# Thirty-two-column tiles for a second mix and an inverse transform, quarter tiles for the last transform

## The chip, the cores and the metric

The kernel runs on one core of one Trainium2 chip. The time is device microseconds (us) of one execution. TensorE is named PE in the profile and its weight loads PEld; VectorE is DVE, ScalarE is ACT, GpSimd is POOL, and the queue that issues the transfers is SP.

## The reference, cut to what matters

Four spectral mixers run one after the other on an array x of 2 images, 64 x 64 positions and 384 channels, all in float32. The second is followed by a token MLP.

```python
xf = rfft2(x, axes=(1, 2)).reshape(B, H, W // 2 + 1, 8, 48)      # 8 blocks of 48 channels
o1 = act(complex_mix(xf, w1) + b1)                               # relu; gelu in layer 1
o2 = complex_mix(o1, w2) + b2                                    # the "second mix"
o2 = softshrink(o2, 0.01)                                        # not in layer 1
y  = irfft2(o2, s=(H, W), axes=(1, 2)) + x
# layer 1 only: LayerNorm ahead, and behind it y + mlp(layernorm(y)), hidden size 1536
```

In layer 1 only 32 of the 64 row frequencies are kept.

## The kernel before

The work on the spectral layers goes by groups g: one block of 48 channels of one layer with both images, so 8 groups a layer and 32 in all. Layers 0, 2 and 3 are "full" (64 row frequencies, 66 columns of the spectrum a group, cut into 9 slots t of 6 or 8 columns); layer 1 is the "norm" layer (4 slots of 16 columns). The program has three spectral stretches: layer 0, layer 1, and layers 2 and 3 together; the token MLP stands between the second and the third.

One group passes through these steps. f1 (line 504) transforms rows, 64x64 tiles of the array, four in use at once. f2 (line 523) transforms columns, with 128 rows and 48 columns in each half of the array. m1 (line 537) is the first mix; ACT applies the activation into h (line 772). m2 (line 555, or 565 in the norm layer) is the second mix: the slot's h is the stationary operand, 64 columns of it a matmul, and the result goes to one of two banks, 4 and 7. In a full layer DVE limits it (clamp, line 928) and subtracts in four pieces of 64 partitions into u (line 934); in the norm layer DVE copies half and ACT half (lines 939, 783). f5 (line 586) is the inverse column transform, six chunks of 8 channels a group: u is stationary, 64 columns a matmul, two matmuls a channel, one for each half of the array. ACT moves the result to v (line 792). f6 (line 602) is the last transform, eight chunks of 8 image rows a group: 128 rows by 64 columns, two matmuls a chunk; DVE adds it to the residual in xs (line 959) and, in layer 0, takes statistics (line 971). SP stores a pair of groups (a unit of 96 channels) in eight transfers and loads a later unit in eight.

The order on each engine is written out by hand. On PE a slot t of group g is: m1 of slot t-1; one f6 chunk of group g-2; f2 of slot t; where due, f1 of group g+1 (slots 0, 3, 6) and f5 of group g-1 (slots 2 to 7); m2 of slot t-1. PE waits in m2 for the eviction of the slot before last (`spread_of(n - 1)`), and in f6 for DVE's addition of the chunk before. The last two groups of a stretch are drained with two banks in turn (`drains`).

Every instruction of PE is in the program text, unrolled, in the spectral stretches; the MLP is a loop. A float32 matmul of the source appears in the profile as two matmul records and two weight loads.

Of the kernel before, what the change touches and what calls it, by code (L numbers as in the profile page):

```python
# [10 lines left out]
P = 128  # L11
# [35 lines left out]
C_ID, C_D5, C_D5H, C_D6, C_COLS = [C_SIGN + SIGNS + P * n for n in range(5)]  # L47
# [11 lines left out]
class Layer:  # L59

    def __init__(self, index, kh, forward, inverse, act, shrink, norm):
# [3 lines left out]
        self.spread = 2 * BATCH if self.full else BATCH  # L65
        self.first_rows = 1 if self.full else 0
# [37 lines left out]
def spread_of(count):  # L104

    return sum(layer_of(g).spread for g, _ in GROUPS[:count])


def imag_of(count):

    return sum(BATCH for g, _ in GROUPS[:count] if layer_of(g).norm)
# [8 lines left out]
ROW_CHUNKS = [(g, k) for g in range(LAYERS * BLOCKS) for k in range(ROWCHUNKS)]  # L120


def row_bank(g, k):
    return 1 if drains(g, k) and k % 2 else 0


def rows_to_clear(g, k):

    n = ROWCHUNKS * g + k
    earlier = [m for m in range(n) if row_bank(*ROW_CHUNKS[m]) == row_bank(g, k)]  # L130
    return earlier[-1] + 1 if earlier else 0
# [63 lines left out]
def build(nc, x, consts, spectral, lncols, ln1, cols, w1, w2, b2, out):  # L195
    with ExitStack() as ctx:
# [30 lines left out]
        with ExitStack() as scope:  # L227
# [10 lines left out]
            u = sb("u", [P, 2, BLOCK, SPAN + BATCH])  # L238
# [35 lines left out]
        F1_BANKS, M2_BANKS, F6_BANKS = (0, 1), (4, 7), (6, 0)  # L274
        F2_BANK, M1_BANK, F5_BANK = 2, 3, 5
# [14 lines left out]
        u_imag, z_shared = sem("u_imag"), sem("z_shared")  # L290
        centred, xn_ready, rows_ready, sum_ready = sem("centred"), sem("xn_ready"), sem("rows_ready"), sem("sum_ready")
        gained, zf_part, u_part, col_ready = sem("gained"), sem("zf_part"), sem("u_part"), sem("col_ready")
# [52 lines left out]
        def _(sp):  # L345
# [24 lines left out]
            def store_unit(unit):  # L370

                for part in range(PARTS):
                    sp.wait_ge(res_ready, ROWCHUNKS * (2 * unit + 1) + PART_ROWS // ROWCHUNK * (part + 1))
# [103 lines left out]
        def _(pe):  # L477

            def f1(g, k):
# [17 lines left out]
                if leads(g) and g and k == 1:  # L497
                    pe.wait_ge(res_ready, ROWCHUNKS * g)
# [42 lines left out]
            def m2(g, t):  # L541
# [4 lines left out]
                if n >= 2:  # L546
                    pe.wait_ge(u_ready, spread_of(n - 1))
                bank = M2_BANKS[n % 2]
# [11 lines left out]
                if imag_of(n - 1):  # L560
                    pe.wait_ge(u_imag, imag_of(n - 1))
                for q in range(size // BATCH):
                    for a in range(2):
                        col = READY_SECOND + a * BLOCK
                        mm = pe.matmul(ps[a * SIDE:(a + 1) * SIDE, bank, q * BLOCK:(q + 1) * BLOCK],  # L565
                                       h[0:ROWS, n % 2, q * SIDE:(q + 1) * SIDE],
                                       mix[0:ROWS, g % 2, col:col + BLOCK], start=True, stop=True)
                mm.then_inc(m2_done, 1)

            def f5(g, k, bank=F5_BANK, reuse=1):  # L570
# [3 lines left out]
                if k == 0:  # L574
                    if g == 0:
                        pe.wait_ge(s_const, 16)
                    pe.wait_ge(u_ready, spread_of(groups_before(g + 1)))
                    if L.norm:
                        pe.wait_ge(u_imag, imag_of(groups_before(g + 1)))
# [4 lines left out]
                for c in range(CHAN):  # L584
                    for a in range(2):
# [748 lines left out]
```

## Time and profile before

| | |
|---|---|
| time, median of 3 runs | 2082.43 us (2081.65 to 2084.39) |
| profiled execution, its own time | 2080.81 us |
| its span | 2079.0 us |
| PE busy | 1934.2 us, 93% |
| DVE busy | 1175.1 us, 57% |
| ACT busy | 1011.0 us, 49% |
| transfers | 141.05 MB, mean 68 GB/s |
| matmul records | 31104, and as many weight loads |

Matmuls overlap each other, so a record's mean time is longer than the step from one to the next, and a busy PE is not PE at its peak. The word "issue" in the profile is time in which an engine waited for nothing that the profile shows.

### The profile page before, as it was taken

The numbers are of one execution on the slowest core, as the hardware profiler recorded it, in microseconds if no ns is written. First come the engines' busy times: TensorE is split into PE (matmuls) and PEld (weight loads), VectorE is DVE, ScalarE is ACT, GpSimd is POOL, SyncE is SP. The second block draws the span as 40 slices with busy tenths as digits, with TensorE's granted clock in tenths as the row PEclk, the third lists the DMA queues.
The fourth block names the chain that finished last, engine by engine and source line by source line (L and its number), as shares of the span: only waits on it lengthen the run. The fifth ranks groups of instructions, "written<-read, shape, count | busy, mean of one in ns | idle before, by whom it ended". The sixth has DMA issues, their size and how long they took to land.

```text
span 2079.0 us, 68971 instructions
## 1 busy us (share of the span) xinstructions
PE 1934.2 (93%) x31104; PEld 1581.3 (76%) x31104; DVE 1175.1 (57%) x2480; ACT 1011.0 (49%) x1644; POOL 434.7 (21%) x425
## 2 busy tenths in 40 slices
PE   5999995698998999999999999999899999999997
PEld 4777672576776999999999999999677777777774
DVE  3687887987855433333333333332467667666675
ACT  3766545576753333333333333333466556655652
POOL 3212103975721000000000000000321121211200
PEclk9999996799998999999999999999999999999998
DMA  9424728307444111111111111114813555457214
GB/s 169 92 49 84 128 58 140 59 8 125 117 103 98 31 31 31 31 30 30 30 30 30 30 30 30 30 31 73 130 16 68 91 101 103 70 86 127 60 36 95
DMA packets 299701, 141.05 MB, mean 68 GB/s; under 512 B 275760, under 2 KB 298032, under 8 KB 299440
## 3 DMA queue, kind: packets, MB, share of 16 engines
q1 hardware_dynamic: 299440, 137.08, 35.9%
q8 instruction: 224, 3.67, 0.8%
q14 instruction: 37, 0.30, 0.0%
HBM read 74.14 MB, written 62.91 MB: 66 GB/s over the span
## 4 chain that ended last, share of the span: by engine, by line
PE 81%; DVE 9%; ACT 3%; issue 2%; POOL 2%; DMA 2%; SPq 1%; DVEq 0%; POOLq 0%; ACTq 0%
PE ps L690 19%; PE ps L675 19%; PE ps L523 9%; PE ps L586 8%; PE ps L537 8%; PE ps L602 7%; PE ps L555 5%; PE ps L504 4%; DVE u L934 3%; DVE st L971 2%; PE ps L565 1%; DVE xs L959 1%; PE ps L660 1%; ACT zf L749 1%; POOL xs L1180 1%
## 5 line engine op out<-in xcount | busy, mean ns | idle before, releaser
L1083 DVE TENSOR_TENSOR gl<-g,gh 128x512 fp32r<-128x512 f32 x192 | 156.8, 817 | 476.4 <-ACT gh L869 476.4
L934 DVE TENSOR_TENSOR u<-ps,clamp 64x192 f32<-64x192 f32 (+1 forms) x864 | 377.0, 436 | 27.7
L866 ACT ACTIVATE g<-ps,colp 128x512 f32<-128x512 f32 x192 | 132.3, 689 | 529.4 <-PE ps L675 529.4
L523 PEld LDWEIGHTS ps<-const,z 128*48 128x48 f32 x8384 | 266.6, 124 | 117.2 <-issue 107.2
L729 ACT ACTIVATE z<-ps 64x512 f32<-64x512 f32 x366 | 234.6, 641 | 113.4 <-PE ps L504 106.6
L523 PE MATMUL ps<-const,z 128*48 128x64 f32 (+1 forms) x8384 | 271.5, 217 | 14.0 <-issue 9.0
L1170 POOL COPY xn<-xs 128x512 f32<-128x512 f32 x144 | 151.2, 1088 | 552.7 <-PE ps L504 364.3
L690 PE MATMUL ps<-w2h,gh 128*128 128x384 f32 x768 | 261.8, 341 | 0.0
L690 PE MATMUL ps<-w2h,gl 128*128 128x384 f32 x768 | 258.5, 337 | 0.0
L690 PE MATMUL ps<-w2l,gh 128*128 128x384 f32 x768 | 257.5, 335 | 0.0
L537 PE MATMUL ps<-zf,w 112*64 112x512 f32 (+2 forms) x992 | 248.3, 574 | 5.9 <-ACT zf L749 1.3
L602 PE MATMUL ps<-v,const 128*64 128x384 f32 x1024 | 219.0, 507 | 21.8 <-DVE xs L959 19.4
L928 DVE TENSOR_SCALAR clamp<-ps 128x384 f32<-128x384 f32 (+1 forms) x216 | 112.6, 521 | 219.3 <-PE ps L555 218.6
L586 PE MATMUL ps<-const,u 128*64 128x64 f32 x6144 | 219.4, 225 | 13.5 <-DVE u L939 6.4
L675 PE MATMUL ps<-mth,w1h 128*128 128x512 f32 x576 | 225.0, 391 | 4.0 <-DVE mtl L1071 4.0
L675 PE MATMUL ps<-mth,w1l 128*128 128x512 f32 x576 | 228.1, 396 | 0.0
L675 PE MATMUL ps<-mtl,w1h 128*128 128x512 f32 x576 | 227.8, 396 | 0.0
L772 ACT ACTIVATE h<-ps,w 113x512 f32<-113x512 f32 (+1 forms) x248 | 162.7, 656 | 122.5 <-PE ps L537 120.1
L586 PEld LDWEIGHTS ps<-const,u 128*64 128x64 f32 x6144 | 199.8, 139 | 29.1 <-ACT v L792 7.5
L749 ACT ACTIVATE zf<-ps 112x512 f32<-112x512 f32 (+1 forms) x216 | 121.3, 561 | 145.1 <-PE ps L523 144.7
L555 PE MATMUL ps<-w,h 113*64 113x96 f32 x3168 | 173.8, 248 | 10.5 <-issue 6.2
L602 PEld LDWEIGHTS ps<-v,const 128*64 128x64 f32 x1024 | 71.2, 139 | 142.8 <-issue 74.1
(70 smaller groups left out, 2516.2 us busy)
## 6 DMA issues: line engine op xcount, KB each, us to landing
after<-xs SPq DMA_DIRECT2D x96, 384.0 KB, 5.4
xs<-after SPq DMA_DIRECT2D x94, 384.0 KB, 8.9
after<-om SPq DMA_DIRECT2D x32, 384.0 KB, 4.3
out<-xs SPq DMA_DIRECT2D x32, 384.0 KB, 5.4
xm<-after SPq DMA_DIRECT2D x30, 384.0 KB, 6.3
xs<-in_x SPq DMA_DIRECT2D x24, 384.0 KB, 8.4
wstage<-in_spectral SPq DMA_DIRECT2D x16, 210.0 KB, 5.7
xs<-in_x SPq DMA_DIRECT2D x4, 768.0 KB, 11.9
```

Of the source, the lines that this page charges most:

```text
L523: mm = pe.matmul(ps[a * SIDE:a * SIDE + BLOCK, F2_BANK, n * L.kh:(n + 1) * L.kh], z[:, g % 2, slot, :], basis(col + a * SIDE, L.kh), start ...
L537: mm = pe.matmul(ps[rows, M1_BANK, 0:width], w[unit % 2][0:MIX, g % 2, rows], zf[0:MIX, n % 2, 0:width], start=True, stop=True)
L555: mm = pe.matmul(ps[b * SIDE:(b + 1) * SIDE, bank, p * PAIR:(p + 1) * PAIR], h[0:ROWS, n % 2, c * SIDE:(c + 1) * SIDE], mix[0:ROWS, g % 2, ...
L586: mm = pe.matmul(ps[a * SIDE:(a + 1) * SIDE, bank, c * SIDE:(c + 1) * SIDE], u[:, g % 2, k * CHAN + c, BATCH * a:BATCH * a + SPAN], basis( ...
L602: mm = pe.matmul(ps[a * SIDE:(a + 1) * SIDE, F6_BANKS[row_bank(g, k)], 0:ROWCHUNK * BLOCK], basis(C_D6 + a * SIDE, SIDE), v[:, g % 2, rows ...
L675: mm = pe.matmul(ps[:, MM1_BANKS[n % 2], :], a[:, at], b[r][:, k, :], start=k == 0 and m == 0, stop=k == KC - 1 and m == 2)
L690: mm = pe.matmul(ps[:, MM2_BANKS[j], 0:CHANNELS], a[:, n % 4, part], b[:, at], start=n == 0 and m == 0, stop=n == HC - 1 and m == 2)
L729: act.activation(to, data, ACT.Copy, scale=layer_of(g).forward).then_inc(z_ready, 1)
L772: act.activation(h[0:ROWS, n % 2, 0:width], ps[0:ROWS, M1_BANK, 0:width], L.act, bias=w[g // 2 % 2][0:ROWS, g % 2, READY_BIAS:W_ALL]).then ...
L934: dve.tensor_tensor(u[to, g % 2, :, start + b:start + size:BATCH], whole, limited, ALU.subtract).then_inc(u_ready, 1)
L1083: dve.tensor_tensor(gl[:, n % 4, :], g[:, n % 2, :], gh[:, n % 4, :], ALU.subtract).then_inc(g_low, 1)
L1170: pool.tensor_copy(xn[:, n % RING], channels(g, k)).then_inc(xt_ready, 1)
```

## The change

Second mix: each matmul covers 32 stationary columns instead of 64 and one half (48) of the 96 output columns, so a column of the slot takes four matmuls, one on each quarter of the array's columns; the result lies with real and imaginary part on the partitions, images side by side. One bank, 4, takes every slot, and PE waits for the eviction of the slot just before. DVE then subtracts in one instruction of 128 partitions; in the norm layer ACT copies all of it in one, and DVE only adds the mean term. Inverse column transform: 32 stationary columns a matmul, four matmuls a channel instead of two. Last transform: except in the drains, two chunks (sixteen rows) a call, each image on its own half of the array's rows, four 64x64 tiles in banks 6 and 7; DVE adds in four pieces of 64 partitions. Calls of f6 move: in a full layer to slots 0, 1, 4 and 8, behind f2 and ahead of f1. Layout constants follow.

```diff
-        F1_BANKS, M2_BANKS, F6_BANKS = (0, 1), (4, 7), (6, 0)
-        F2_BANK, M1_BANK, F5_BANK = 2, 3, 5
+        F1_BANKS, F6_BANKS = (0, 1), (6, 7)
+        F2_BANK, M1_BANK, M2_BANK, F5_BANK = 2, 3, 4, 5
...
 def rows_at(g, t):
...
     if not layer_of(g).full:
-        return [(g - 2, 2 * t), (g - 2, 2 * t + 1)]
-    if t == layer_of(g).n - 1:
-        return [(g - 1, 0)]
-    return [(g - 2, t + 1)] if t < ROWCHUNKS - 1 else []
+        return [(g - 2, 2 * t)]
+    return {0: [(g - 2, 2)], 1: [(g - 2, 4)], 4: [(g - 2, 6)], layer_of(g).n - 1: [(g - 1, 0)]}.get(t, [])
...
                 if L.full:
                     for c in range(size):
-                        p, b = c // BATCH, c % BATCH
                         col = READY_SECOND if start + c < SPAN else MINUS
-                        mm = pe.matmul(ps[b * SIDE:(b + 1) * SIDE, bank, p * PAIR:(p + 1) * PAIR],
-                                       h[0:ROWS, n % 2, c * SIDE:(c + 1) * SIDE],
-                                       mix[0:ROWS, g % 2, col:col + PAIR], start=True, stop=True)
+                        for a in range(2):
+                            for k in (0, HALF):
+                                mm = pe.matmul(ps[a * SIDE + k:a * SIDE + k + HALF, bank, c * BLOCK:(c + 1) * BLOCK],
+                                               h[0:ROWS, n % 2, c * SIDE + k:c * SIDE + k + HALF],
+                                               mix[0:ROWS, g % 2, col + a * BLOCK:col + (a + 1) * BLOCK],
+                                               start=True, stop=True)
...
                 for q in range(size // BATCH):
-                    for a in range(2):
-                        col = READY_SECOND + a * BLOCK
-                        mm = pe.matmul(ps[a * SIDE:(a + 1) * SIDE, bank, q * BLOCK:(q + 1) * BLOCK],
-                                       h[0:ROWS, n % 2, q * SIDE:(q + 1) * SIDE],
-                                       mix[0:ROWS, g % 2, col:col + BLOCK], start=True, stop=True)
+                    for b in range(BATCH):
+                        for a in range(2):
+                            col, to = READY_SECOND + a * BLOCK, b * SIDE + a * HALF
+                            mm = pe.matmul(ps[to:to + HALF, bank, q * BLOCK:(q + 1) * BLOCK],
+                                           h[0:ROWS, n % 2, (q * BATCH + b) * HALF:(q * BATCH + b + 1) * HALF],
+                                           mix[0:ROWS, g % 2, col:col + BLOCK], start=True, stop=True)
...
                 for c in range(CHAN):
-                    for a in range(2):
-                        mm = pe.matmul(ps[a * SIDE:(a + 1) * SIDE, bank, c * SIDE:(c + 1) * SIDE],
-                                       u[:, g % 2, k * CHAN + c, BATCH * a:BATCH * a + SPAN],
-                                       basis((C_D5 if L.full else C_D5H) + a * SIDE, SIDE),
-                                       start=True, stop=True)
+                    for b in range(BATCH):
+                        for a in range(2):
+                            to = b * SIDE + a * HALF
+                            mm = pe.matmul(ps[to:to + HALF, bank, c * SIDE:(c + 1) * SIDE],
+                                           u[:, g % 2, k * CHAN + c, b if L.full else 0, a:a + HALF],
+                                           basis(C_D5 + a * SIDE if L.full else C_D5H + (b * 2 + a) * SIDE, SIDE),
+                                           start=True, stop=True)
...
+                for c in range(2):
+                    rows = slice((k + c) * ROWCHUNK, (k + c + 1) * ROWCHUNK)
+                    for b in range(BATCH):
+                        mine = slice(b * SIDE, (b + 1) * SIDE)
+                        mm = pe.matmul(ps[c * SIDE:(c + 1) * SIDE, F6_BANKS[b], 0:ROWCHUNK * BLOCK],
+                                       const[mine, C_D6 + b * SIDE:C_D6 + (b + 1) * SIDE],
+                                       v[mine, g % 2, rows, :].rearrange("p h c -> p (h c)"), start=True, stop=True)
+                mm.then_inc(f6_done, 2)
...
-                    for b, a in ((0, 0), (0, 1), (1, 1), (1, 0)):
-                        mine, to = slice(b * SIDE, (b + 1) * SIDE), slice(a * SIDE, (a + 1) * SIDE)
-                        whole, limited = (d[mine].rearrange("p (s a c) -> p a c s", a=2, c=BLOCK)[:, a]
-                                          for d in (data, part))
-                        dve.tensor_tensor(u[to, g % 2, :, start + b:start + size:BATCH], whole, limited,
-                                          ALU.subtract).then_inc(u_ready, 1)
+                    whole, limited = (d.rearrange("p (k b c) -> p c b k", b=BATCH, c=BLOCK) for d in (data, part))
+                    first = start // BATCH
+                    dve.tensor_tensor(u[:, g % 2, :, :, first:first + size // BATCH], whole, limited,
+                                      ALU.subtract).then_inc(u_ready, 1)
...
+                dve.wait_ge(f6_done, n + 2)
+                for c in range(2):
+                    for b in range(BATCH):
+                        to = residual(g, (k + c) * ROWCHUNK, ROWCHUNK)[b * SIDE:(b + 1) * SIDE]
+                        data = ps[c * SIDE:(c + 1) * SIDE, F6_BANKS[b], 0:ROWCHUNK * BLOCK]
+                        dve.tensor_tensor(to, data.rearrange("p (h c) -> p h c", c=BLOCK), to, ALU.add).then_inc(res_ready, 1)
```

## Rows read from the trace of the kernel before

**Rows 1.** The page: engines, instruction queue, chain that ended last by line.
```profile
PE 1934.2 (93%) x31104; PEld 1581.3 (76%) x31104; DVE 1175.1 (57%) x2480; ACT 1011.0 (49%) x1644; POOL 434.7 (21%) x425
...
q8 instruction: 224, 3.67, 0.8%
...
PE ps L690 19%; PE ps L675 19%; PE ps L523 9%; PE ps L586 8%; PE ps L537 8%; PE ps L602 7%; PE ps L555 5%; PE ps L504 4%; DVE u L934 3%; DVE st L971 2%; PE ps L565 1%; DVE xs L959 1%; PE ps L660 1%; ACT zf L749 1%; POOL xs L1180 1%
```

**Rows 2.** Windows: start:end, length, busy (count) of PE, PEld, DVE, ACT, POOL; clock, DMA, GB/s.
```profile
40.00:310.00 270.00, 255.61 (x6062) 191.92 (x6060) 209.49 (x574) 161.66 (x263) 46.47 (x61) 1.00 0.47 86
416.00:468.00 52.00, 49.65 (x1510) 39.08 (x1506) 42.96 (x49) 39.49 (x66) 37.62 (x28) 0.99 0.04 9
1505.20:2045.00 539.80, 523.75 (x12540) 398.41 (x12538) 369.41 (x792) 325.76 (x530) 94.07 (x114) 1.00 0.44 77
```

**Rows 3.** Chain that ended last, in order of time: start us, us, what.
```profile
1601.60 1.09 PE ps L504 x64
1602.69 1.08 PE ps L586 x32
1603.77 0.66 PE ps L555 x16
1604.43 0.86 PE ps L537 x4
1605.30 0.67 PE ps L523 x24
1605.97 0.93 PE ps L586 x32
1606.90 0.66 PE ps L555 x16
1607.57 0.65 PE ps L537 x4
1608.21 0.65 PE ps L602 x4
```

**Rows 4.** Timeline of PE around one stop: start us, us, group, idle before.
```profile
1629.22 0.22 PE L523 MATMUL ps<-const,z 128*48 128x64 f32 x1
1630.94 1.04 PE L523 MATMUL ps<-const,z 128*48 128x64 f32 x30 [1.50 <-issue]
```

**Rows 5.** Windows from one such point to the next, columns as in rows 2.
```profile
1612.08:1618.12 6.04, 4.65 (x135) 3.57 (x131) 3.43 (x9) 4.21 (x7) 1.95 (x6) 1.00 1.30 193
1618.12:1624.62 6.50, 6.49 (x127) 5.14 (x127) 4.24 (x10) 2.57 (x4) 0.00 (x0) 1.00 1.32 183
1624.62:1630.93 6.31, 4.82 (x134) 3.49 (x128) 4.01 (x9) 3.78 (x6) 0.52 (x1) 1.00 0.72 102
...
477.37:481.54 4.17, 3.84 (x134) 3.05 (x130) 4.14 (x4) 2.85 (x5) 2.30 (x3) 1.00 0.44 83
...
1955.67:1959.18 3.51, 3.35 (x135) 3.02 (x130) 1.62 (x4) 2.10 (x5) 1.48 (x2) 1.00 0.60 131
```

**Rows 6.** DMA in the window 1630.94 to 1632.00.
```profile
DMA packets 0, 0.00 MB, mean 0 GB/s; under 512 B 0, under 2 KB 0, under 8 KB 0
```

**Rows 7.** DMA in the window 1632.05 to 1633.30, with its queue.
```profile
DMA packets 1, 0.02 MB, mean 13 GB/s; under 512 B 0, under 2 KB 0, under 8 KB 0
...
q8 instruction: 1, 0.02, 6.2%
```

**Rows 8.** Groups by shape, DVE, PE and PEld: busy us, mean ns, idle before.
```profile
L934 DVE TENSOR_TENSOR u<-ps,clamp 64x192 f32<-64x192 f32 x576 | 281.2, 488 | 18.5
...
L959 DVE TENSOR_TENSOR xs<-ps,xs 128x384 f32<-128x384 f32 x256 | 141.6, 555 | 42.7 <-PE ps L602 36.5
...
L928 DVE TENSOR_SCALAR clamp<-ps 128x384 f32<-128x384 f32 x144 | 80.1, 556 | 177.5 <-PE ps L555 177.1
```

**Rows 9.** Groups by shape, PE: the norm layer's second mix, and f2 there.
```profile
L523 PE MATMUL ps<-const,z 128*48 128x32 f32 x2048 | 52.9, 210 | 4.2 <-issue 2.4 <-DVE z L915 1.8
...
L565 PE MATMUL ps<-w,h 113*64 113x48 f32 x1024 | 38.0, 227 | 0.6 <-issue 0.5
```

More of the change, by code:

```diff
@@ L46 @@
 C_D2, C_D2A, C_D2B, C_SIGN = [SPAN + P * n for n in range(4)]
-C_ID, C_D5, C_D5H, C_D6, C_COLS = [C_SIGN + SIGNS + P * n for n in range(5)]
+C_ID, C_D5, C_D5H, C_D6, C_COLS = [C_SIGN + SIGNS + P * n for n in (0, 1, 2, 4, 5)]
 ROWS = ONE_ROW + 1
@@ L101, with full_before, norm_before @@
 GROUPS = [(g, t) for g in range(LAYERS * BLOCKS) for t in range(LAYER[g // BLOCKS].n)]
[L104 to L111, printed above, removed]
+def full_before(count):
+    return sum(layer_of(g).full for g, _ in GROUPS[:count])
+def norm_before(count):
+    return sum(layer_of(g).norm for g, _ in GROUPS[:count])
 def drains(g, k):
@@ L117, in drains @@
     return g == last - 1 or g == last - 2 and k >= layer_of(g).first_rows
-ROW_CHUNKS = [(g, k) for g in range(LAYERS * BLOCKS) for k in range(ROWCHUNKS)]
-def row_bank(g, k):
-    return 1 if drains(g, k) and k % 2 else 0
 def rows_to_clear(g, k):
     n = ROWCHUNKS * g + k
-    earlier = [m for m in range(n) if row_bank(*ROW_CHUNKS[m]) == row_bank(g, k)]
-    return earlier[-1] + 1 if earlier else 0
+    before = (g, k - 1) if k else (g - 1, ROWCHUNKS - 1)
+    return n - 1 if drains(g, k) and drains(*before) else n
 def shrunk_before(g):
@@ L545, in m2 @@
                 pe.wait_ge(h_ready, n + 1)
-                if n >= 2:
-                    pe.wait_ge(u_ready, spread_of(n - 1))
-                bank = M2_BANKS[n % 2]
+                if n and layer_of(GROUPS[n - 1][0]).full:
+                    pe.wait_ge(u_ready, full_before(n))
+                elif n:
+                    pe.wait_ge(u_copied, norm_before(n))
+                bank = M2_BANK
                 mix = w[g // 2 % 2]
@@ L620, in spectral @@
                         behind = at_slot(L.f5_at, t) if g > first else []
-                        for r in rows[0:1]:
-                            f6(*r)
                         f2(g, t)
                         if L.full:
+                            for r in rows:
+                                f6(*r)
                             for k in ahead:
@@ L628, in spectral @@
                             f5(g - 1, k)
-                        for r in rows[1:]:
-                            f6(*r)
                         if not L.full:
+                            for r in rows:
+                                f6(*r)
                             for k in ahead:
@@ L778, in m2 @@
                 act.wait_ge(m2_done, groups_before(g) + t + 1)
-                bank = M2_BANKS[(groups_before(g) + t) % 2]
-                start, size = L.groups[t]
-                for b in range(BATCH):
-                    part = slice(SIDE + b * HALF, SIDE + (b + 1) * HALF)
-                    act.activation(u[HALF:SIDE, g % 2, :, start + b:start + size:BATCH],
-                                   ps[part, bank, 0:size // BATCH * BLOCK].rearrange("p (s c) -> p c s", c=BLOCK),
-                                   ACT.Copy).then_inc(u_imag, 1)
+                start, size = (n // BATCH for n in L.groups[t])
+                act.activation(u[:, g % 2, :, 0, start:start + size],
+                               ps[:, M2_BANK, 0:size * BLOCK].rearrange("p (s c) -> p c s", c=BLOCK),
+                               ACT.Copy).then_inc(u_copied, 1)
             def f5(g, k, bank=F5_BANK):
```

94 lines of the change are left out of this document (47 added, 47 removed).

## The prediction

> **What bounds the kernel now.** I read the page's engine line and chain first [rows 1]. PE is 93% busy and its lines hold nearly all of the chain; the three changed steps (L586, L602, L555) hold 20% of it, and DVE's u and xs 4%. The token MLP (L675, L690) is untouched. So the change is worth what it does to PE in the spectral stretches. The windows say the same [rows 2]: 12,540 matmul records in 539.8 us of layers 2 and 3, with PE 97% busy and DVE 68%.
>
> A full group has 848 records: f1 192, f2 264, m1 36, m2 132, f5 192, f6 32 (two for each matmul of the source). So that window holds 14.8 groups of 36.5 us. Layer 0 gives 6,062 / 848 = 7.15 groups in 270 us, 37.8 each. A norm group has 192 + 256 + 16 + 128 + 192 + 32 = 816, so 1,510 records in 52 us are 1.85 groups of 28.1 us [rows 2].
>
> The chain in order of time prices the steps [rows 3]: f1 1.09, f5 1.08 behind f1 and 0.93 elsewhere, m2 0.66 for a slot of eight, m1 0.86 for a slot of eight, f2 0.67 for a slot of six, f6 0.65 a chunk. A group's own work is 3 x 1.09 + 11 x 0.67 + 8.25 x 0.86 + 8.25 x 0.66 + 3 x 1.08 + 3 x 0.93 + 8 x 0.65 = 34.4 us. The other 2.1 us are stops.
>
> **Where those stops come from.** The timeline shows PE stopping in the middle of f2, waiting for nothing ("issue"), for 1.50 us [rows 4]. It names no engine, so I counted instructions between such points [rows 5]: each stretch holds 128 matmul records and 128 weight loads, within a few records that straddle the edge. So these are borders of 256-instruction blocks. The instruction queue moved 224 packets of 3.67 MB [rows 1]: 16.4 KB each, 64 bytes for each of 256 instructions. I read this as PE refilling its program block by block, one block ahead.
>
> The price of a refill is in two answers. After the stop that ended at 1630.94 there is no packet at all until 1632.00, with the DMA empty [rows 6]; then one instruction packet alone [rows 7]. Asked for when the block begins, it thus starts over 1.06 us later. The shortest block that ends in a stop took 3.51 us, a longer one 4.17 [rows 5]. While a unit's eight loads fill the DMA, three blocks in a row took 6.04, 6.50 and 6.31 [rows 5]: the packet queues behind the loads. Now a block is 256 / 1,696 of a group, 5.5 us of work, so only load bursts stop PE.
>
> **The change, part by part.**
>
> *Second mix, full layers.* 66 columns x 4 matmuls x 2 = 528 records in place of 132. Each streams 48 columns in place of 96 through a quarter in place of half of the array. If quarters run side by side as halves do, a slot of eight costs 16 rounds of 41 ns = 0.66 us, as now (0.66 / 16 records = 41 ns, two at once, so 82 ns for 96 columns) [rows 3]. No row has four quarters of 128 rows. The lower bound is 0.66. Nearest above is f1, four tiles at once, 1.09 / 64 = 17 ns a record, so 1.09; two at a time would be 1.32. I take 0.66, because f1 shows four tiles at once and holds twice the stationary columns.
>
> *Inverse transform.* 16 x 2 x 2 = 64 records a chunk in place of 32. f2, with 48 stationary columns, streams 64 at 0.67 / 24 = 28 ns for two at once, 56 a round; 16 rounds are 0.89, against 0.93 [rows 3]. Bounds: 0.89 and 1.79 (two at a time). I take 0.89.
>
> *Last transform.* Four matmuls, eight records of 384 columns on four tiles, cost for sixteen rows what two halves cost for eight: 0.65. The group saves 4 x 0.65 = 2.6 us [rows 3].
>
> *Changes of tile shape.* f5 behind f1 costs 0.15 more than behind f2 [rows 3]. I take that as the price of going between 64x64 and 128x64 tiles. Before, six changes a group (around three f1). After, f2 and m1 use halves, f6 and f1 64x64 tiles, f5 and m2 quarters: three changes in slots 0, 1, 3, 4, 6, 8, two in the others, 24. That is 18 more, 2.7 us; if halves to quarters is free, nearly nothing.
> The Trainium skill's TensorEngine Tiling (Array Packing), Key Properties, says that changing the tiling mode, as opposed to the tile, drains TensorE. The trace agrees for 64x64 against 128x64 (0.15 us) and shows no quarters; by the rule all 24 count, and without it for quarters the group's own work would be some 2 us less.
>
> Own work of a full group after it: f1 3 x 0.94 (its changes taken out) = 2.8, f2 7.4, m1 7.1, m2 5.4, f5 6 x 0.89 = 5.3, f6 2.6, together 30.6, and 24 changes x 0.15 = 3.6: 34.2, as before. A norm group: 2.6 less for f6 and 0.7 for f5. Its m2 has 37 ns a record of busy time [rows 9], 1.2 us a slot, against 0.66; four slots make 2.1 at most, of which I take half, since busy time holds tails that overlap. Nine changes more are 1.4: 28.1 - 4.4 + 1.4 = 25.1.
>
> *Evictions.* DVE's four subtractions of 0.488 become one of 128 partitions, 0.56 if as the addition at L959, 0.98 if 384 elements cost twice 192; the four additions for sixteen rows cost 4 x 0.56 in place of 2 x 0.56 [rows 8]. A group gains over 4 us of DVE, which isn't the bound. One bank makes m2 wait for the slot just before. Its eviction takes some 1.1 us and a slot 3.7, so it's ready. In layer 0, behind an f6 pair and 16 statistics, it is up to 1.4 us late four times in half of the groups; the stops below cover that. PE's f6 wait is a slot long, so free. No transfer is added or moved.
>
> *Refills, the term that decides.* A full group gets 848 + 396 + 192 = 1,436 records, 2,872 instructions, 11.2 blocks in place of 6.6. A norm group 816 + 128 + 192 = 1,136, 8.9 in place of 6.4. Own work per block falls to 34.2 / 11.2 = 3.1 us and 25.1 / 8.9 = 2.8, below the 3.51 that a refill takes. So PE's rate becomes one block a refill. I take 3.7, between 3.51 and 4.17 and near the first, and 6.3 in a load burst of three blocks.
>
> A full unit (two groups) with a burst: 22.4 blocks, 3 x 6.3 + 19.4 x 3.7 = 90.7, and 1.7 for slots 8, 0 and 1, whose own work is about 4.0 a block: 92.4 us. Without a burst 84.6. Twelve full units, nine with bursts: 9 x 92.4 + 3 x 84.6 = 1,085 us, against 16 x 36.5 + 8 x 37.8 = 886: +199. Norm: 71 blocks x 3.7 + 3 x 2.6 = 271, against 225: +46. The last f5 of three stretches: 384 more instructions each, +9. Sum +254. On the profiled execution's own 2,081 (1.6 under the median, nothing here) that is **2,335 us**, 12% slower.
>
> **The rivals.**
> A. *Refills don't set the rate* (fetched further ahead when blocks pass faster). For it: the trace never shows two blocks in a row at this pace. Against: the stops at exact borders, and the empty DMA before the packet of rows 7. Then own work decides: full groups the same, norm groups 8 x 3.0 = 24 less, f6's waits and layer 0's DVE load some 15 less: 2,040, faster. It decides if a block can be had in under 3.0 us.
> B. *Quarters don't overlap four at a time.* m2 1.32 and f5 1.79 put full groups' own work at 34.2 + 5.4 + 5.4 = 45.0, 4.0 a block; with burst excess 3 x 2.3 / 2 = 3.5 that is 48.6, +12 x 24 = 288, norm groups 25.1 + 8 = 33, about +50: 2,420.
> The skill's TensorE: Matmul & The Clock Gate, Measured speedup vs the span model, has three column tiles of 32 at 2.38 times one. No run here shows it; it speaks against B.
> C. *Refill limit met only in part*, since PE's queue runs ahead of its work so that requests go out sooner. At 3.4 a block for 340 blocks, 100 us less: 2,235. With sparse slots recovering more, 2,180.
> D. *The two sides cancel*: own work gains of the last transform just pay for refills, 2,080. It needs 3.2 a block in quiet stretches and a shape change at nothing.
>
> **How the numbers follow.** Refills as summed 0.66, C 0.17 (both slower), B 0.07 (slower), A 0.07 (faster), D 0.03 (same). The range takes the refill price from 3.3 to 4.0 a block (340 x 0.4 = 136 below, 340 x 0.3 = 102 above): 2,200 to 2,437, which holds C's first figure and B too. Faster by over 0.2% (about what a measurement of this kernel can tell from no change) 0.07, same 0.03, slower 0.90.
>
> **What would show it.** Right: some 350 instruction packets in place of 224; windows of 128 and 128 records of about 3.7 us over whole groups, with "issue" before PE at their ends; PE busy in the third stretch well under 90%; m2 0.66 to 0.7, f5 0.9 to 1.05, f6 0.65 for sixteen rows; L934 216 times in place of 864, DVE's share down. Wrong: blocks under 3.3 us in a row (A, C), m2 over 1.1 a slot (B), or PE waiting for DVE's u or xs.

## The result and the profile after

| | before | after |
|---|---|---|
| time, median of 4 runs each | 2082.04 us (2076.76 to 2084.39) | 2386.85 us (2379.22 to 2390.78) |
| span of the profiled execution | 2079.0 us | 2377.4 us |
| ratio of the times | | 1.146, 95% interval 1.143 to 1.150 |

The change makes the kernel 15% slower: +305 us, where +254 was forecast.

The page of the kernel after: span, engines, instruction queue and the chain that ended last.

```profile
span 2377.4 us, 101827 instructions
...
PE 2013.3 (85%) x47776; PEld 1621.1 (68%) x47776; DVE 1073.8 (45%) x1988; ACT 993.5 (42%) x1612; POOL 435.6 (18%) x425
...
q8 instruction: 354, 5.80, 1.0%
...
PE 77%; issue 11%; DVE 8%; ACT 1%; DMA 1%; SPq 1%; POOL 0%; DVEq 0%; POOLq 0%; ACTq 0%
```

Against [rows 1], matmul records go from 31,104 to 47,776 and instruction packets from 224 to 354. DVE and ACT have less work (1175.1 to 1073.8 us and 1011.0 to 993.5), POOL as much as before, and PE's busy share falls from 93% to 85%. "issue" now holds 11% of the chain, where it held 2%.

Waits of PE, kernel after (line, what it waited for, us in total, times, longest), the first four and one more:

```profile
PE ps L548 <- issue: 98.1, 61, 4.8
PE ps L583 <- issue: 63.4, 55, 4.5
PE ps L513 <- issue: 46.7, 49, 3.5
PE ps L548 <- DVE u L934: 24.3, 22, 3.1
...
PE ps L494 <- issue: 18.6, 18, 3.4
```

"issue" stands before m2 (L548), f5 (L583), f2 (L513) and f1 (L494) alike. It goes with the place in the program, not with a step. Counted from the records of the trace, stops of 0.3 us or more at 256-instruction borders, from the start of one record to the start of the next, make 37.5 us before (32 stops) and 288.7 us after (210 stops). The profile's own idle time of PE put down to "issue", which leaves out the record still running, sums to 34.9 us before and 245.4 after. So by the one measure 251 us of the 298 by which the span grew are such stops, by the other 210. The spectral stretches have some 340 borders; at 130 of them PE doesn't stop.

Windows of five blocks in a row in a quiet stretch, kernel after, columns as in rows 2:

```profile
1903.40:1907.23 3.83, 3.83 (x128) 2.51 (x127) 1.41 (x2) 2.56 (x5) 0.53 (x1) 1.00 0.02 4
1907.24:1910.57 3.33, 2.56 (x130) 1.83 (x128) 2.23 (x4) 1.17 (x2) 0.00 (x0) 1.00 0.02 5
1910.58:1913.93 3.35, 3.35 (x128) 2.61 (x127) 1.40 (x2) 1.36 (x3) 0.00 (x0) 1.00 0.02 5
1913.94:1917.41 3.47, 3.47 (x140) 2.62 (x128) 1.41 (x2) 1.80 (x3) 0.00 (x0) 1.00 0.02 5
1917.41:1921.05 3.64, 2.07 (x130) 1.86 (x127) 0.00 (x0) 2.56 (x4) 2.13 (x2) 1.00 0.02 5
```

Before, the trace had no two blocks of this pace in a row. Now they follow each other at 3.3 to 3.8 us, with the DMA nearly idle (share 0.02) and clock 1.00. In two of the five PE was busy for little more than half or three quarters of the time (2.07 of 3.64, 2.56 of 3.33); in the other three it was busy throughout, so there its own work set the pace. The timeline of PE shows what this looks like inside a slot:

```profile
1908.94 0.85 PE L548 MATMUL ps<-w,h 113*32 113x48 f32 x61
1910.59 0.28 PE L548 MATMUL ps<-w,h 113*32 113x48 f32 x3 [0.79 <-issue]
```

61 of the 64 records of a slot's m2 run. The last three stand in the next block and come 0.79 us late.

The chain in order of time around it gives the steps' own prices (start us, us, what):

```profile
1903.93 0.68 PE ps L548 x60
...
1910.86 1.00 PE ps L527 x3
1911.86 0.90 PE ps L513 x32
1912.76 1.03 PE ps L583 x64
1913.79 0.78 PE ps L548 x64
```

The last four lines are m1, f2, f5 and m2 of one slot of eight; the first is an m2 without its last records. DVE's new subtraction, by shape:

```profile
L934 DVE TENSOR_TENSOR u<-ps,clamp 128x384 f32<-128x384 f32 x144 | 120.7, 838 | 5.0
```

Now whole groups. These windows run from the first f1 record (a weight load) of a group to that of the next, so each holds one group (some 1,436 records):

```profile
1791.30:1833.90 42.60, 36.86 (x1444) 27.11 (x1440) 19.99 (x33) 22.49 (x37) 8.28 (x12) 1.00 0.02 5
1833.90:1888.80 54.90, 41.11 (x1441) 30.66 (x1437) 20.51 (x35) 22.20 (x36) 6.52 (x6) 0.91 0.67 122
1888.80:1930.40 41.60, 37.44 (x1440) 27.32 (x1436) 20.61 (x35) 22.18 (x36) 8.28 (x12) 1.00 0.02 5
1930.40:1983.60 53.20, 39.44 (x1444) 28.67 (x1440) 21.25 (x36) 22.21 (x36) 6.49 (x6) 0.95 0.71 126
```

The same for the kernel before:

```profile
1724.10:1759.40 35.30, 35.09 (x854) 26.48 (x852) 24.75 (x54) 22.14 (x36) 6.36 (x6) 1.00 0.55 111
1759.40:1796.90 37.50, 35.57 (x854) 27.13 (x852) 24.80 (x54) 22.13 (x36) 8.24 (x12) 1.00 0.53 75
```

Before, the transfers of a unit spread over both of its groups (DMA share 0.55 and 0.53) and cost 2 us. After, they fall into one group, which takes 53 to 55 us where its quiet neighbour takes 42.

Here is where the 298 us of span lie, by the first f1 record of each group, with the forecast for the same stretch by the prediction's own terms (46.2 us a group of a unit with a burst, 42.3 of one without, over 37.8 in layer 0 and 36.5 in layers 2 and 3):

| stretch | before | after | more | forecast |
|---|---|---|---|---|
| layer 0, start to group 4 | 130.6 | 161.1 | +30.5 | +34 |
| groups 4 to 6, two with transfers after | 110.5 | 154.1 | +43.6 | +25 |
| group 7 to the first norm m2 | 145.0 | 166.5 | +21.5 | +11 |
| norm layer and its drain | 257.8 | 297.3 | +39.5 | +49 |
| MLP | 816.4 | 816.1 | -0.3 | 0 |
| last stretch, its first four groups | 116.8 | 147.2 | +30.4 | +23 |
| its groups 20 to 29 | 368.1 | 472.1 | +104.0 | +97 |
| group 30 to the end | 133.8 | 163.0 | +29.2 | +15 |

The rows' borders are records of PE, so the first steps of the norm layer count in the row ahead of it.

### The profile page after: what moved, and what is told of

It is laid out like the page before. It is cut to its first block, busy times and chain, and to the rows that moved or that the text cites. A ratio compares the mean times of both kernels' runs of the same rounds, so it can differ in the third digit from the quotient of the medians.

```text
span 2377.4 us, 101827 instructions
## 1 busy us (share of the span) xinstructions
PE 2013.3 (85%) x47776; PEld 1621.1 (68%) x47776; DVE 1073.8 (45%) x1988; ACT 993.5 (42%) x1612; POOL 435.6 (18%) x425
## 4 chain that ended last, share of the span: by engine, by line
PE 77%; issue 11%; DVE 8%; ACT 1%; DMA 1%; SPq 1%; POOL 0%; DVEq 0%; POOLq 0%; ACTq 0%
PE ps L697 17%; PE ps L682 17%; PE ps L527 9%; PE ps L513 9%; PE ps L583 9%; PE ps L548 6%; PE ps L494 4%; PE ps L609 4%; DVE xs L966 3%; DVE st L982 2%; PE ps L558 1%; PE ps L600 1%; PE ps L667 1%; DVE xn L1002 1%; DVE u L934 1%
## 5 line engine op out<-in xcount | busy, mean ns | idle before, releaser
L513 PEld LDWEIGHTS ps<-const,z 128*48 128x48 f32 x8384 | 286.3, 130 | 199.0 <-issue 193.2
L513 PE MATMUL ps<-const,z 128*48 128x64 f32 (+1 forms) x8384 | 297.6, 224 | 51.7 <-issue 46.7
L548 PE MATMUL ps<-w,h 113*32 113x48 f32 x12672 | 203.5, 210 | 124.9 <-issue 98.1
L966 DVE TENSOR_TENSOR xs<-ps,xs 64x384 f32<-64x384 f32 x424 | 235.4, 555 | 145.5 <-PE ps L609 135.3
L583 PE MATMUL ps<-const,u 128*32 128x64 f32 x12288 | 237.4, 226 | 65.9 <-issue 63.4
L548 PEld LDWEIGHTS ps<-w,h 113*32 113x32 f32 x12672 | 171.3, 112 | 169.1 <-issue 155.1
L527 PE MATMUL ps<-zf,w 112*64 112x512 f32 (+1 forms) x992 | 272.5, 622 | 3.6 <-issue 3.4
L583 PEld LDWEIGHTS ps<-const,u 128*32 128x32 f32 x12288 | 196.5, 113 | 109.2 <-issue 86.9
L494 PE MATMUL ps<-const,xn 64*64 64x64 f32 x6144 | 129.5, 237 | 64.5 <-POOL xn L1179 23.8
L796 ACT ACTIVATE v<-ps 128x512 f32<-128x512 f32 x192 | 114.6, 597 | 165.2 <-PE ps L583 164.1
```

The lines of the kernel that those rows point to most:

```text
L494: mm = pe.matmul(ps[j * SIDE:(j + 1) * SIDE, banks[b], c * SPAN:(c + 1) * SPAN], xn[rows, slot, first + j, :], const[rows, C_D1:C_D1 + SPA ...
L513: mm = pe.matmul(ps[a * SIDE:a * SIDE + BLOCK, F2_BANK, n * L.kh:(n + 1) * L.kh], z[:, g % 2, slot, :], basis(col + a * SIDE, L.kh), start ...
L527: mm = pe.matmul(ps[rows, M1_BANK, 0:width], w[unit % 2][0:MIX, g % 2, rows], zf[0:MIX, n % 2, 0:width], start=True, stop=True)
L548: mm = pe.matmul(ps[a * SIDE + k:a * SIDE + k + HALF, bank, c * BLOCK:(c + 1) * BLOCK], h[0:ROWS, n % 2, c * SIDE + k:c * SIDE + k + HALF] ...
L583: mm = pe.matmul(ps[to:to + HALF, bank, c * SIDE:(c + 1) * SIDE], u[:, g % 2, k * CHAN + c, b if L.full else 0, a:a + HALF], basis(C_D5 + ...
L966: dve.tensor_tensor(to, data.rearrange("p (h c) -> p h c", c=BLOCK), to, ALU.add).then_inc(res_ready, 1)
```

## The experiments

**Empty instructions.** The first two runs were to fill PE's program with instructions that do nothing, in the kernel before: as many as the change adds, and half as many.

```diff
+            def pad(count):
+                for _ in range(count):
+                    pe.nop(nofuse=True)
...
+                        pad(12)    # per matmul of m2 in a full layer; 4 in the norm layer, 4 in f5 (half: 6, 2, 2)
```

> The kernel before, with empty instructions (no operation) put behind the matmuls of m2 and f5 on PE, so many that a full group has 2,872 PE instructions and a norm group 2,272, as in the changed kernel, at the same places. No tile shape, no bank, no eviction and no wait changes. Refill theory (PE's program comes in blocks of 256 instructions, one block ahead, some 3.5 us each): nearly the changed kernel's time, 2,330 to 2,420 us, with some 350 instruction packets and stops at block borders. Rival (quarter tiles, changes of tile shape and the single bank are what costs): 2,082 to 2,100. If the empty instructions themselves are slow on the sequencer (50 ns as a semaphore instruction's row has), over 2,500, with PE idle inside m2 and f5 and not at block borders.

> The same with half as many empty instructions: 2,284 a full group, 8.9 blocks. Refill theory: own work is 3.9 us a block on the mean but dense blocks fall under 3.5, so part of the price: 2,140 to 2,190, far less than half of what full padding adds. A fixed price per instruction: half of what the full padding adds. Rival of shapes and bank: 2,082.

Measured: 0.9995 (0.9983 to 1.0007) and 1.0002 (0.9985 to 1.002) of before. But the page of the first shows that its program was no longer than before:

```profile
PE 1932.4 (93%) x31104; PEld 1581.6 (76%) x31104; DVE 1174.1 (56%) x2480; ACT 1011.6 (49%) x1644; POOL 436.1 (21%) x425
...
q8 instruction: 224, 3.67, 0.8%
```

224 packets, as in [rows 1]: the empty instructions were not in the program that ran. Neither run speaks for or against refills. They are two repeats of the kernel before, which agree with it within 0.1%. The instructions had to be real ones.

**Tiny matmuls.** In the kernel after, one matmul of one column by one is added per column of the spectrum in m2 (full layers) and two per channel in f5. Each writes an element that the matmul behind it overwrites.

```diff
+                                if (2 * a + k // HALF) == c % 4:
+                                    to = a * SIDE + k
+                                    pe.matmul(ps[to:to + 1, bank, c * BLOCK:c * BLOCK + 1],
+                                              h[0:ROWS, n % 2, c * SIDE + k:c * SIDE + k + 1],
+                                              mix[0:ROWS, g % 2, col:col + 1], start=True, stop=True)
...
+                            if c % 2 == a:
+                                pe.matmul(ps[to:to + 1, bank, c * SIDE:c * SIDE + 1],
+                                          u[:, g % 2, k * CHAN + c, b if L.full else 0, a:a + 1],
+                                          basis(C_D5, 1), start=True, stop=True)
```

> The padding with empty instructions told nothing, since they were not in the program that ran (224 instruction packets, as before). So instructions that do run: the changed kernel with tiny matmuls added ahead of real ones, one stationary and one moving column each, on the same quarter, into an element that the real one then overwrites; one for each column of m2 in a full layer and two for each channel of f5. A full group gets 66 + 96 of them, 648 PE instructions, 2.5 blocks more, a norm group 384, 1.5 blocks. Refill theory: 24 x 2.5 x 3.5 + 8 x 1.5 x 3.5 = 250 us over the changed kernel where nothing hides them, less where blocks are already longer than a refill: 2,550 to 2,640, and some 425 packets. Rival (own work sets the time): a record on a quarter steps by 11 ns in m2, so 324 records are 3.6 us a group, 24 x 3.6 + 8 x 2.1 = 103: 2,490 at most.

Measured: 2668.75 us, 1.280 (1.274 to 1.285). A quiet group in windows, and the page:

```profile
q8 instruction: 427, 7.00, 1.1%
```

```profile
2180.90:2232.60 51.70, 41.00 (x1764) 31.07 (x1760) 20.53 (x35) 22.13 (x36) 8.20 (x12) 0.97 0.02 5
```

That is 29 us over the upper edge of what I expected. 73 packets more than after come with 282 us more, 3.9 us a packet. The tiny matmuls aren't free for PE: counted from the records where nothing stops, a chunk of f5 takes 1.13 us in place of 0.92 and m2 of a slot of eight 1.01 in place of 0.82, some 2.8 us a full group and 78 in all (an estimate). The granted clock is 0.938 against 0.955 as well, and PE was busy for 271.5 us at the low level in place of 164.2, which at half speed is at most 54 us. The two together are less than half of the 282. The quiet group holds 1,760 / 128 = 13.75 blocks in 51.7 us, 3.76 each; the quiet group of the kernel after holds 11.2 in 41.6, 3.71 each. Stops at the borders grow from 288.7 to 465 us (counted from the records), which is 176 of the 282. So the rival by which PE's own work sets the time (2,490 at most) falls.

**The inverse transform alone.** The kernel before with f5 on quarters, and the layout of u and of the constant that goes with it; two banks, old m2, old f6.

```diff
-                    for a in range(2):
-                        mm = pe.matmul(ps[a * SIDE:(a + 1) * SIDE, bank, c * SIDE:(c + 1) * SIDE],
-                                       u[:, g % 2, k * CHAN + c, BATCH * a:BATCH * a + SPAN],
+                    for b in range(BATCH):
+                        for a in range(2):
+                            to = b * SIDE + a * HALF
+                            mm = pe.matmul(ps[to:to + HALF, bank, c * SIDE:(c + 1) * SIDE],
+                                           u[:, g % 2, k * CHAN + c, b, a:a + HALF],
...
```

> The kernel before with the inverse transform alone on quarters (and the layout of u and of the last transform's constant that this needs); second mix and last transform as before, two m2 banks. 2,080 PE instructions a full group, 2,016 a norm group. Refill theory: own work rises little (twelve changes of shape, 1.8 us a group, less 0.2), and dense blocks (f1, f5, m2 in a row) fall under a refill: 60 to 110 us over before, 2,140 to 2,190. Rival (the single bank and the second mix on quarters cost): 2,080 to 2,125.

Measured: 2156.17 us, 1.036 (1.032 to 1.041), with 272 packets. The chain in order of time around a stop:

```profile
1701.51 0.89 PE ps L523 x32
1702.40 1.03 PE ps L588 x64
1703.43 0.81 PE ps L555 x16
...
1708.77 0.31 PE ps L555 x2
1709.08 1.24 issue
1710.31 0.79 PE ps L555 x13
```

This is within what I expected. The border stops take 75 us against 37.5, by the same count. The rest of the +74 is in the steps. f5 (L588) takes 1.03 against 0.93 behind f2, and the unchanged m2 on halves (L555) 0.81 behind it against 0.66 [rows 3]. Going from quarters to halves costs those 0.15 us too.

**One bank.** The kernel before, with m2 on bank 4 only and waiting for the eviction of the slot just before.

```diff
-        F1_BANKS, M2_BANKS, F6_BANKS = (0, 1), (4, 7), (6, 0)
+        F1_BANKS, M2_BANKS, F6_BANKS = (0, 1), (4, 4), (6, 0)
...
-                if n >= 2:
-                    pe.wait_ge(u_ready, spread_of(n - 1))
+                if n:
+                    pe.wait_ge(u_ready, spread_of(n))
...
```

> The kernel before with one bank for m2 in place of two, so that PE waits for the eviction of the slot just before; nothing else. Its eviction is four subtractions there, 2.6 us with the limit. m2_halves showed 100 us of PE waiting for DVE's u behind one bank. Theory: this bank is what m2_halves lost beside refills: 40 to 100 us over before, 2,120 to 2,180. Rival (two banks were slack, as the prediction had it for the one subtraction of 0.84 us): 2,080 to 2,090.

Measured: 2109.69 us, 1.012 (1.008 to 1.016): +28 us, between the two ranges that I had expected. PE's first wait:

```profile
PE ps L555 <- DVE u L934: 40.3, 61, 1.5
```

With four subtractions, the eviction of the slot before is not always done: 61 waits, up to 1.5 us. In the changed kernel, with one subtraction, the same wait stands 22 times for 24.3 us: 13 times in layer 0 for 21.0 us, the longest 3.1, and in layers 2 and 3 eight times for 1.6 us together.

**The second mix back on halves.** The kernel after with m2 of the full layers on halves, four subtractions of 64 partitions, still one bank.

```diff
-                        for a in range(2):
-                            for k in (0, HALF):
-                                mm = pe.matmul(ps[a * SIDE + k:a * SIDE + k + HALF, bank, c * BLOCK:(c + 1) * BLOCK],
+                        p, b = c // BATCH, c % BATCH
+                        mm = pe.matmul(ps[b * SIDE:(b + 1) * SIDE, bank, p * PAIR:(p + 1) * PAIR],
...
```

> The changed kernel with the second mix of the full layers back on halves of the array (64 stationary and 96 moving columns, four subtractions of 64 partitions on DVE), the rest as changed, still one bank. 2,080 PE instructions a full group in place of 2,872; PE's own work nearly the same, DVE's longer. Refill theory: most of the loss goes, 2,120 to 2,170. Rival (inverse and last transform on new shapes, or the single bank, cost): stays over 2,300.

Measured: 2244.21 us, 1.079 (1.077 to 1.081), 280 packets. So 74 packets and 143 us less than after, but 74 to 124 us more than I expected. The border stops are down to 117 us, as the theory has it. What I had left out is in the first row of PE's waits:

```profile
PE ps L547 <- DVE u L935: 100.3, 109, 3.8
```

With four subtractions per slot, four additions per sixteen rows and one bank, PE waits 100 us for DVE's u, half of it in layer 0 (50.1 us). DVE holds 25% of the chain, where it held 9% before.

**The last transform back on halves.** The kernel after, sixteen rows a call, but each chunk on two 128x64 halves; DVE adds in two pieces of 128 partitions.

```diff
                     for b in range(BATCH):
-                        mm = pe.matmul(ps[c * SIDE:(c + 1) * SIDE, F6_BANKS[b], 0:ROWCHUNK * BLOCK],
-                                       const[mine, C_D6 + b * SIDE:C_D6 + (b + 1) * SIDE],
-                                       v[mine, g % 2, rows, :].rearrange("p h c -> p (h c)"), start=True, stop=True)
+                        mm = pe.matmul(ps[b * SIDE:(b + 1) * SIDE, F6_BANKS[c], 0:ROWCHUNK * BLOCK],
+                                       basis(C_D6 + b * SIDE, SIDE), v[:, g % 2, rows, :].rearrange("p h c -> p (h c)"),
+                                       start=True, stop=True)
```

> The changed kernel with the last transform on halves of the array (128 rows by 64 columns, sixteen rows a call still, both banks), so 1.29 us of PE a call in place of 0.65 by the records of 384 columns, with as many instructions as before the edit. Refill theory: PE has slack in blocks that hold f6, but dense blocks don't hold it, so part of 2.6 us a group shows: 30 to 50 us over the changed kernel (2,417 to 2,437). If own work set the time: 32 groups x 2.6 = 83 over, less the saved changes of shape. If the last transform's time were wholly covered by refills: the same.

Measured: 2401.32 us, 1.153 (1.152 to 1.155), 354 packets: 14 us more than after, less than the 30 to 50 that I had expected. PE is busy for 51 us more (2064.3 against 2013.3). That is 106 calls at 0.48: the chain has 1.29 us a call on halves, and 0.81 on four tiles, with the change of shape in it. So what is at stake is 51 us and not 83, and 14 of them are seen (27 in the two profiled executions). The stops don't become shorter: "issue" sums to 245.4 us in both. PE's wait for u in m2 falls from 24.3 to 8.2 us, since DVE adds in two pieces in place of four; the rest I can't place. At least here, an edit that shortens PE's work by 51 us and leaves the number of instructions was worth 14.

**Both back on halves.** The two edits above together, with one bank.

> The changed kernel with second mix (full layers) and last transform both back on halves; sixteen rows a call and one bank stay. As many instructions as m2_halves, PE's own work 2.6 us a group longer, but DVE has two additions of 128 partitions a call in place of four of 64, 1.1 us less ahead of m2's eviction. If the one bank behind a long DVE queue is what m2_halves lost: as fast or faster than it, 2,210 to 2,245. If own work counts: 40 to 80 slower.

Measured: 2207.35 us, 1.058 (1.053 to 1.062), 280 packets. This has more PE work than the run with m2 alone back, and is 37 us faster, because DVE's two additions free its queue: m2's wait for u falls from 100.3 to 36.4 us. With 74 packets less than after, it is 180 us faster. Against the run before this one, from which it differs in m2 alone, it is 194 us faster, 2.6 a packet. What remains over before is f5's 48 packets and the shape changes (+74 by themselves), the norm layer's 8 packets, and the one bank (+28 by itself). These add up to 2082 + 74 + 28 = 2,184; the last 23 us I did not take apart.

**Loads spread out.** In the kernel before, and then in the kernel after, a unit's eight loads are issued one for each f2 slot in place of all at once.

```diff
-            def load_unit(unit):
+            def load_unit(unit, behind=None):
                 for part in range(PARTS):
                     for b in range(BATCH):
+                        if behind is not None:
+                            n = part * BATCH + b
+                            sp.wait_ge(f2_done, groups_before(behind) - 1 + (n if layer_of(behind).full else n // 2))
                         load_rows(unit, b, part)
...
-                        load_unit(unit + 3)
+                        load_unit(unit + 3, 2 * unit + 4)
```

> The kernel before with the eight loads of a unit issued one behind each slot of f2 (two a slot in the norm layer) in place of all at once; where a unit is loaded late in a stretch the loads spread over some 30 us in place of 14. Theory: the three blocks of a load burst that take 6.3 us, since the instruction packet queues behind the loads, shrink to under 5, so the stops of some 1.5 us behind them go: 10 to 25 us less, 2,057 to 2,072. Rival: the loads come late for POOL's copies of x into xn and f1 waits: slower, 2,090 or more. Rival: the stops only move: same.

> The changed kernel with the same pacing of loads. Theory: blocks in bursts lose 6.4 - 3.5 us each, three to four a unit, in about ten units: 60 to 90 us less, 2,300 to 2,325. Rival (bursts only shift where blocks wait): within 10 us of the changed kernel.

Measured: 2067.82 us for the kernel before with spread loads, 0.994 (0.992 to 0.995), faster than both kernels and as expected; and 2375.33 us for the kernel after, 1.140 (1.138 to 1.142), 11 us less than after. The same window around the burst of [rows 5], first of before, then with spread loads:

```profile
1605.00:1640.00 35.00, 32.01 (x738) 24.67 (x734) 23.33 (x52) 19.35 (x32) 6.11 (x10) 1.00 0.73 115
```

```profile
1605.00:1640.00 35.00, 34.10 (x830) 26.30 (x826) 23.88 (x52) 21.58 (x36) 7.87 (x12) 1.00 0.50 93
```

830 matmul records in place of 738 in 35 us. PE's "issue" sums to 26.8 us in place of 34.9, which is 8 of the 14 us. Blocks of 5.5 us have slack, and a packet that is only a little late fits into it. In the kernel after the same edit makes the groups alike instead of shorter. Four in a row:

```profile
1744.20:1790.00 45.80, 37.95 (x1440) 28.48 (x1436) 21.14 (x36) 21.89 (x36) 6.37 (x6) 0.96 0.45 95
1790.00:1836.40 46.40, 37.17 (x1443) 27.16 (x1439) 20.15 (x34) 22.51 (x37) 8.04 (x12) 1.00 0.26 55
1836.40:1884.80 48.40, 37.97 (x1440) 28.39 (x1436) 20.58 (x35) 22.20 (x36) 6.47 (x6) 0.96 0.41 89
1884.80:1929.90 45.10, 38.72 (x1440) 29.09 (x1436) 20.59 (x35) 22.25 (x36) 8.13 (x12) 0.96 0.26 57
```

A pair takes 92 to 94 us, where the three middle pairs of a loaded and a quiet group take 95 to 97 without it. I had expected 60 to 90 us of gain; there is no slack left in which a late packet could hide, so the delay only moves.

## Why the prediction was right, point by point

**Refills set the rate: shown, in some two thirds of the blocks.** 354 packets against "some 350". PE is busy for 581.4 of 705 us in layers 2 and 3 (1640 to 2345), 82%: "well under 90%". The times of the programs line up with their packets: 224 gives 2,068 to 2,110 us, 272 gives 2,156, 280 gives 2,207 and 2,244, 354 gives 2,375 to 2,401, 427 gives 2,669. The tiny matmuls separate this from the other parts of the change, apart from their own work and the clock, under half of the 282. Rival A (blocks had in under 3.0 us) falls with the five blocks of 3.3 to 3.8 in a row, and D with it; C's 3.4 a block is met by single blocks, not by the mean.

**3.7 us a quiet block: right.** It gives 42.3 us for a quiet group. The trace has 40.9 to 43.4 for the ten quiet full groups. Counted from the records, the 62 quiet blocks that begin and end in a stop take 3.64 us (median; most lie between 3.3 and 4.1), so this is the price of a refill. But two in five quiet blocks end in no stop and take 3.8 us on the mean, by PE's own work; the forecast had every block held by its refill.

**Quarters run four at a time: right, rival B falls.** m2's 64 records take 0.67 to 0.68 us from first to last, f5's 0.88. The chain's 1.03 holds a change of shape as well. Its 0.78 for m2 follows none, since f5 too is on quarters; these 0.1 us I can't explain.

**A change of shape costs 0.15 us, halves to quarters too: right.** This was the choice between counting 24 changes and fewer. m1 takes 1.00 us in place of 0.86 when it follows quarters, f5 1.03 in place of 0.88, and in the run with f5 alone an unchanged m2 took 0.81 in place of 0.66. The Trainium skill's TensorEngine Tiling (Array Packing), Key Properties, has the drain for any change of the tiling mode; the trace agrees, for quarters as well. The slot of the chain above takes 1.00 + 0.90 + 1.03 + 0.78 = 3.71 us, where the forecast's terms give 0.86 + 0.89 + 0.89 + 0.66 + 2 x 0.15 = 3.60. So PE's own work is what was forecast, within 3%, and the loss is in refills.

**Where the size was off.** The term that was mis-sized is "6.3 in a load burst of three blocks", which makes a loaded group 42.3 + 7.8 = 50.1 us. Of the seven groups with the transfers of a whole unit, five took 53.2 to 56.8, one 50.8 and one 48.9. Blocks of one of them, in windows:

```profile
1834.68:1839.68 5.00, 3.98 (x143) 2.67 (x136) 4.31 (x9) 3.66 (x6) 2.20 (x2) 1.00 0.93 190
1843.14:1848.34 5.20, 3.39 (x127) 2.53 (x127) 1.40 (x2) 1.88 (x3) 0.00 (x0) 1.00 0.64 151
...
1864.00:1869.06 5.06, 5.06 (x127) 4.19 (x130) 1.40 (x2) 1.46 (x3) 0.15 (x1) 0.66 0.69 141
1869.06:1875.62 6.56, 3.03 (x143) 2.23 (x133) 1.40 (x2) 3.08 (x5) 2.04 (x2) 0.98 1.31 186
1875.62:1881.81 6.19, 3.48 (x128) 3.19 (x127) 0.00 (x0) 1.73 (x3) 0.00 (x0) 0.74 1.30 192
1881.81:1888.82 7.01, 6.67 (x125) 3.96 (x129) 4.02 (x7) 2.14 (x4) 0.00 (x0) 0.76 0.09 15
```

The first two lie in the stretch in which the unit is stored. The forecast priced the loads alone. I had read their cost from a kernel in which a block holds 5.5 us of work and so covers the 5.0 to 5.2 us that one takes beside stores. Once blocks want 3 us, the stores stop PE as well. A block ahead of the loads, beside the load of the mix weights and two stores, takes 4.99. The blocks of 6.56 and 6.19 are the forecast's 6.3: their packets start 3.6 and 3.3 us after the block, in place of 1.2 in quiet blocks (counted from the records).

The two others, 5.06 and 7.01, aren't held by a refill at all. No stop stands at their ends, PE is busy for 5.06 and 6.67 us in them, and in the second the DMA is nearly idle (0.09). Their clock is 0.66 and 0.76: PE runs at the 1.2 GHz level for 3.4 us of each, behind stops of 2.97 and 2.71 us. The chain in order of time shows it:

```profile
1861.03 2.97 issue
...
1865.28 1.69 PE ps L513 x32
1866.97 1.83 PE ps L494 x64
1868.81 1.03 PE ps L583 x64
...
1882.10 1.29 PE ps L527 x3
1883.39 1.28 PE ps L513 x24
1884.67 1.35 PE ps L609 x8
```

f2 of a slot of eight takes 1.69 us in place of 0.90 and f1 1.83 in place of 1.09 [rows 3]; behind the second stop m1, f2 and f6 of a slot of six take 1.29, 1.28 and 1.35 in place of 0.79, 0.67 and 0.81. These five steps alone are 3.2 us, a quarter of the 12.6 by which this group is over 42.3. So a long stop that the clock follows costs a second time. The prediction has no term for this.

Even the three blocks that I read for the 6.3 weren't all of one kind: the middle one, 6.50, holds 6.49 us of PE's work [rows 5] and ends in no stop. Only 6.04 and 6.31 were set by a refill.

In the table the mis-sized term is 13 of the +19 over the forecast in groups 4 to 6 (56.3 and 56.8 against 50.1 each), and +12 in groups 20 to 29, of which the quiet groups (41.9 against 42.3) and before's own price (36.8 against 36.5) take 5 back.

The rest of the miss lies at both ends of a stretch. The forecast took 36.5 us as before's price for every group, but the first ones have no f6 yet and took 29.2 and 32.6 us for the same blocks, which now take 41.4 and 43.4 (groups 17 and 18, first f1 record to the next); the row of the first four groups is 7 over. From group 30 to the end and from group 7 to the norm layer it is +14 and +10 over the forecast; in these, drains and a stretch with stores come together, and I did not tell them apart. The norm layer was forecast 10 us too dear. Its price after was right: its six middle groups take 33.5 us each, against 271 / 8 = 33.9. Before's 28.1, which I had read from one window of 52 us, was 30.4 over the same six groups. The sum's +9 for the last f5 of three stretches counts twice, since 1,436 and 1,136 records a group already hold it; as the measured time is over the forecast, this hid a part of the miss.

**One bank: small, but not covered in layer 0.** Outside layer 0 the prediction's "so it's ready" nearly holds: 1.6 us of waits in layers 2 and 3. For layer 0 it had waits of up to 1.4 us that "the stops below cover", and nothing in the sum; there it is 21.0 us in 13 waits, the longest 3.1. The wait is +28 us in the kernel before by itself, with four subtractions. The eviction is 0.56 + 0.84 = 1.4 us of DVE's time behind whatever stands in its queue, not 1.1, since the strided subtraction of 128 partitions takes 838 ns, between the bounds of 0.56 and 0.98 and nearer the upper.

**The clock: left out.** The granted clock is 0.955 over the kernel, against 0.976 before. It is 0.96 to 1.00 in quiet groups and 0.90 to 0.97 in loaded ones. Over the whole execution PE was busy for 164.2 us at the 1.2 GHz level, against 54.4 before (counted from the clock's rows and PE's records). Work at half speed loses half of its time, so the difference makes some 55 us (an estimate), and less where a refill would have held PE anyway. No run sets the clock apart, so its share of the +298 stays open below that.

## What to carry to other kernels

An unrolled program has a price for each instruction, also for one that costs PE next to nothing: here 256 of them must hold some 3.6 us of work, and 5 to 6.6 us while transfers run. Before splitting a matmul into more and smaller tiles, divide each stretch's time by its instructions; a stretch that lands under that price gets slower however well the tiles overlap. And a cost that was read where there was slack (a burst, a buffer) has to be read again for a kernel that has none.

## What the runs showed of the hardware

- Four column tiles of 32 with 113 rows of the array in use stream 48 columns each in 0.67 us for 16 rounds, 42 ns a round, as two tiles of 64 do with 96 columns.
- The packet for the next block doesn't start before the present block does, even when many blocks in a row stop PE. Over the 62 quiet blocks that begin and end in a stop it starts 1.2 us after the block's start, takes 1.0, and PE goes on 1.4 us after it has landed (medians). Behind the start of the quiet block at 1903.40 the DMA has no packet from 1903.45 to 1904.45, and from there to 1905.6 the one instruction packet alone.
- PE's granted clock falls behind long stops. Between 1640 and 2345, ten of its twelve falls stand beside a stop of PE of 2.5 to 4.8 us (counted from the clock's rows and PE's records), while the 1.40 and 1.50 us stops of the kernel before, in the burst of [rows 5], left it at 1.00. In the block from 1869.06, PE was busy for 3.03 of 6.56 us at 0.98; in the next one, with 3.48 of 6.19, it was 0.74, a mixture of the 2.4 and 1.2 GHz levels. Back in dense work at 1888.8 it is 1.00. At the lower level f2 took 1.69 us in place of 0.90 and f1 1.83 in place of 1.09.
- DVE's subtraction from a bank with a strided read of 384 elements on 128 partitions takes 838 ns, where the limit (clamp) over the same elements takes 558.
